# An attention layer's last block: three groups of heads finished in a chain of their own

## What is computed

```
x = x + attention(layernorm(x))     # 16 heads of 16, rotary positions, causal softmax, w_proj and b_proj
x = x + ffn(layernorm(x))
ffn(y) = sqrt((y @ cos(theta + theta_noise))**2 + (y @ sin(phi + phi_noise))**2)
```

## Time and profile before

| | |
|---|---|
| median of 3 runs | 1975.45 us (1974.7 to 1977.72) |
| the profiled execution, own time / span | 1979.04 / 1977.3 us |
| PE busy | 1939.0 us, 98% |
| DVE busy | 1559.9 us, 79% |
| ACT busy | 1389.1 us, 70% |
| POOL busy | 871.0 us, 44% |
| chain that ended last | PE 87%, ACT 5% |
| mean granted TensorE clock | 0.997 |

### The profile page before, as it was taken

How to read it: one execution, slowest core, us unless ns; L and a number is a source line. 1 busy time by engine, 2 the same in 40 slices (tenths; PEclk the granted TensorE clock), 3 DMA queues, 4 the chain that set the end, 5 groups by cost and what they waited for, 6 DMA issues and landing times.

```text
span 1977.3 us, 38203 instructions
## 1 busy us (share of the span) xinstructions
PE 1939.0 (98%) x12036; PEld 798.1 (40%) x12036; DVE 1559.9 (79%) x4101; ACT 1389.1 (70%) x2687; POOL 871.0 (44%) x1336
## 2 busy tenths in 40 slices
PE   7999999999999999999999999999999999999998
PEld 4333433334443434343443443434444344433335
DVE  5898789988778787887877878888777877879725
ACT  3466668877676777877767777777767767777883
POOL 4714615443535454633544435553444545431232
PEclk9999999999999999999999999999999999999999
DMA  6301312122121221311222121322212212120131
GB/s 143 97 24 28 121 47 73 39 71 65 52 73 54 74 83 64 105 35 64 61 71 77 57 72 56 104 68 71 72 33 71 68 64 78 51 94 7 49 105 57
DMA packets 130762, 133.30 MB, mean 67 GB/s; under 512 B 29434, under 2 KB 105722, under 8 KB 130554
## 3 DMA queue, kind: packets, MB, share of 16 engines
q1 hardware_dynamic: 127728, 128.29, 21.1%
q10 hardware_dynamic: 2832, 2.56, 0.7%
HBM read 38.49 MB, written 25.68 MB: 32 GB/s over the span
## 4 chain that ended last, share of the span: by engine, by line
PE 87%; ACT 5%; issue 2%; DVE 2%; DMA 2%; POOL 1%; SPq 0%; DVEq 0%; POOLq 0%; ACTq 0%
PE banks L1094 23%; PE banks L1079 23%; PE banks L1057 22%; PE banks L1012 6%; PE banks L1001 6%; ACT probs L1198 3%; PE banks L1039 3%; PE banks L946 2%; DVE chunk_max L1399 1%; PE banks L935 1%; DMA squares<-sums 1%; PE banks L928 1%; PE banks L1065 0%; DVE banks L1394 0%; PE banks L1024 0%
## 5 line engine op out<-in xcount | busy, mean ns | idle before, releaser
L1198 ACT ACTIVATE probs<-banks 128x512 f32<-128x512 f32 (+1 forms) x2240 | 1143.9, 602 | 328.6 <-PE banks L1079 289.3
L1399 DVE TENSOR_REDUCE chunk_max<-banks 128x1 f32<-128x512 f32 x1536 | 985.3, 683 | 216.7 <-PE banks L1057 215.0
L1079 PE MATMUL banks<-queries,stack_k 99*128 99x512 bf16 (+3 forms) x2560 | 740.5, 350 | 11.8 <-ACT probs L1198 4.1
L1057 PE MATMUL banks<-stack_k,queries 96*128 96x512 bf16 (+3 forms) x2560 | 712.2, 349 | 8.2 <-DMA queries<-parts 2.8
L1394 DVE CUSTOM_DVE_ANT_0 banks<-banks,row_mask 128x128 f32<-128x128 f32 (+3 forms) x1024 | 483.7, 508 | 87.4 <-PE banks L1057 86.8
L1094 PE MATMUL banks<-probs,v_one 128*17 128x512 f32 (+3 forms) x5120 | 527.8, 532 | 1.1 <-POOL probs L1526 0.6
L1079 PEld LDWEIGHTS banks<-queries,stack_k 99*128 99x128 bf16 x2560 | 231.4, 97 | 435.9 <-ACT probs L1198 218.7
L1057 PEld LDWEIGHTS banks<-stack_k,queries 96*128 96x128 bf16 x2560 | 233.0, 97 | 310.9 <-DVE chunk_max L1399 67.3
L1526 POOL TENSOR_SCALAR_AFFINE_SELECT probs<-probs 128x512 f32<-128x512 f32 x256 | 160.9, 638 | 402.5 <-ACT probs L1198 402.0
L1094 PEld LDWEIGHTS banks<-probs,v_one 128*17 128x17 f32 x5120 | 119.7, 96 | 266.3 <-issue 173.7
L1394 DVE DVE_READ_ACCUMULATOR2_ANT chunk_max<- 128x1 f32 x1024 | 144.0, 141 | 0.0
(11 more groups left out here) (158 smaller groups left out, 1162.3 us busy)
## 6 DMA issues: line engine op xcount, KB each, us to landing
queries<-parts SPq DMA_DIRECT2D x384, 64.0 KB, 2.6
stack_k<-parts SPq DMA_DIRECT2D x354, 64.0 KB, 2.6
sums<-o_raw SPq DMA_DIRECT2D x64, 256.0 KB, 2.3
rot<-raw SPq DMA_DIRECT2D x236, 64.0 KB, 2.0
xin<-x SPq DMA_DIRECT2D x17, 512.0 KB, 4.2
mid<-x SPq DMA_DIRECT2D x13, 512.0 KB, 5.1
heads_t<-sums SPq DMA_DIRECT2D x26, 256.0 KB
inverse<-inverses SPq DMA_DIRECT2D x26, 256.0 KB
```

The lines of the kernel that those rows point to most:

```text
L1057: mm = nc.tensor.matmul(bank[:, n * wide:(n + 1) * wide], queries[0:SPLIT_ROWS, query_place(u, t), h + n, j * P:(j + 1) * P], stack_k[u % ...
L1079: mm = nc.tensor.matmul(bank[:, a * wide:(a + 1) * wide], stack_k[u % 2][0:ROWS, j // SUB, first + a, (j % SUB) * P:(j % SUB + 1) * P], qu ...
L1198: nc.scalar.activation(probs[:, g % PROBS, first:first + many, w0:SPAN], bank, ACT.Exp).then_inc(s_exp, 1)
L1399: nc.vector.tensor_reduce(to, bank[:, 0:count * wide].rearrange("p (h n) -> p h n", h=count), AX.X, ALU.max).then_inc(s_emptied["DVE"], 1)
```

## The change

`FINAL`'s early jobs (den, heads, x3, bias, invert, keepinv, inverse, scale, the two leads) are tied in the plan to those of the finish before the last batch (`m = n - SPANS`, number 11) in place of number 14's, and get a due time of their own, `LEAD_AT` = 15.3. They have semaphores of their own, since they now overtake 12, 13 and 14, and the denominators' load waits until `stack_k[0]` is free. No computation is added or taken away.

```diff
+LEAD_AT = 15.3
...
-            job(("den", n), "SP", 0.5, at, [stored, ("power", prev, 1), ("sin", KT - 1), ("den", n - 1), begun(at - SLACK)], 2.2)
...
+            m = n - SPANS if n == FINAL else n - 1
+            at = LEAD_AT if n == FINAL else at
+            job(("den", n), "SP", 0.5, at, [stored, ("power", prev, 1), ("sin", KT - 1), ("den", m), begun(at - SLACK), *(free if n == FINAL else [])], 2.2)
+            job(("heads", n), "SP", 1.5, at, [stored, ("wave", prev, SUB - 1), ("sin", KT - 1), ("heads", m), *free], 2.5)
+            job(("x3", n), "SP", 0.65, at, [("final", prev), ("x3", m), begun(at - SLACK), *free], 4.2)
+            job(("bias", n), "POOL", 2.5, at, [("x3", n), ("bias", m)])
...
+            job(("scale", n), "DVE", 1.25, at, [("heads", n), ("inverse", n), ("scale", m)])
             for a in range(2):
                 first = ("lead" if n == FINAL else "proj", n, a)
-                job(first, "PE", 8 * 4 * DIM / 2 / 2400, at + 0.1, [("scale", n), ("proj", n - 1, 1), ("lead", n, 0) if a else ("scale", n)])
+                job(first, "PE", 8 * 4 * DIM / 2 / 2400, at + 0.1, [("scale", n), ("proj", m, 1), ("lead", n, 0) if a else ("scale", n)])
...
-                job(("weights",), "SP", 0.8, at - 0.4, projected, 3.0)
+                job(("weights",), "SP", 0.8, LAST_AT - 0.4, projected, 3.0)
...
+                    if n == FINAL:
+                        take_late(n)
...
-                    pe.wait_ge(s_scaled, FINAL + 1)
+                    pe.wait_ge(s_lead_scaled, 1)
...
-                        dve.wait_ge(s_bias, n + 1)
+                        if n == FINAL:
+                            dve.wait_ge(s_lead_bias, 1)
+                        else:
+                            dve.wait_ge(s_bias, n + 1)
```

More of the change, by code:

```diff
@@ L337, in plan @@
             stored = ("store", unit - (n == FINAL), t)
-            job(("den", n), "SP", 0.5, at, [stored, ("power", prev, 1), ("sin", KT - 1), ("den", n - 1), begun(at - SLACK)], 2.2)
-            job(("heads", n), "SP", 1.5, at, [stored, ("wave", prev, SUB - 1), ("sin", KT - 1), ("heads", n - 1), *free], 2.5)
-            job(("x3", n), "SP", 0.65, at, [("final", prev), ("x3", n - 1), begun(at - SLACK), *free], 4.2)
-            job(("bias", n), "POOL", 2.5, at, [("x3", n), ("bias", n - 1)])
@@ new lines, in plan @@
+            job(("heads", n), "SP", 1.5, at, [stored, ("wave", prev, SUB - 1), ("sin", KT - 1), ("heads", m), *free], 2.5)
+            job(("x3", n), "SP", 0.65, at, [("final", prev), ("x3", m), begun(at - SLACK), *free], 4.2)
+            job(("bias", n), "POOL", 2.5, at, [("x3", n), ("bias", m)])
+            job(("invert", n), "DVE", 0.5, at, [("den", n), ("invert", m)])
+            job(("keepinv", n), "SP", 0.65, at, [("invert", n), ("keepinv", m)], 2.2)
+            job(("inverse", n), "SP", 1.4, at, [("keepinv", n), ("add", prev), ("inverse", m), *free], 6.8)
@@ L614, in layer_kernel @@
         s_scaled = sem("heads_scaled3")
+        s_lead_bias = sem("last_bias_added")
+        s_lead_inverted = sem("last_denominators_of_first_groups_inverted")
+        s_lead_scaled = sem("last_heads_of_first_groups_scaled")
         s_stat3 = sem("stats_chain3")
@@ L811, in keep_inverses @@
                     f = finish_set(n)
-                    sp.wait_ge(s_inverted, n + 1)
+                    if n == FINAL:
+                        sp.wait_ge(s_lead_inverted, 1)
+                    else:
+                        sp.wait_ge(s_inverted, n + 1)
                     count = heads_by_memory(n)
@@ L1296, in invert @@
                     dve.wait_ge(s_den[f], 16 * (same_set(n)[0] + 1))
-                    nc.vector.reciprocal(denominators[f][rows, :], denominators[f][rows, :]).then_inc(s_inverted, 1)
+                    nc.vector.reciprocal(denominators[f][rows, :], denominators[f][rows, :]).then_inc(s_lead_inverted if n == FINAL else s_inverted, 1)
                 def scale_heads(n):
@@ L1306, in scale_heads @@
                         nc.vector.tensor_tensor(heads_t[f][0:rest_rows, 1, :], heads_t[f][0:rest_rows, 1, :], inverse3[f][0:rest_rows, 1, :],
-                                                ALU.mult).then_inc(s_scaled, 1)
+                                                ALU.mult).then_inc(s_lead_scaled, 1)
                         return
@@ L1492, in add_bias @@
                     nc.gpsimd.tensor_tensor(mid[f][:, :, :], mid[f][:, :, :], bias[:, :].unsqueeze(1).to_broadcast([P, SUB, DIM]),
-                                            ALU.add).then_inc(s_bias, 1)
+                                            ALU.add).then_inc(s_lead_bias if n == FINAL else s_bias, 1)
                 def sum_squares(n, a):
```

## The result

The changed kernel takes 1981.42 us, median of 8 runs (1979.05 to 1984.75), beside 1976.69 us for the kernel before, median of 8 (1974.7 to 1977.72). The ratio is 1.0026, interval 1.0016 to 1.0037: slower by 0.26%. The profiled execution has a span of 1978.6 us.

The account below looks back on a forecast made before the run. PE, busy 98% of the span, was taken as the bound. Leads in the body at +4.58 us and the tail at -0.12 made +4.5 on 1975.45, so 1979.9 us; 8-in-10 range 1977.2 to 1981.8.

Parts of the forecast that it names:

- item 2: Unit 15's span 3 up to the last lift: leads on the path, less 0.34 us of PE idle, +4.58 us.
- item 1: The two leads moved from tail to body: 16 records keep their alternation of rows and take 4.92 us there too.
- The rival's 3.46 us: Leads in the body: 16 records at the like-shape pace of 0.216 us, +3.0 us in all, 1978.5; chance 0.04.
- The reserve of scores in ACT: At the second lead: two waiting score banks give ACT 0.9 us of cover; left out of the sum, kept for the range.
- The sign that misled: Last lift of the changed profile: expected 4 to 5 us later, at 1937; under 3 us later would mean the leads hid.
- Where PE is the limit: From 1886 to 1896, behind the leads: ACT busy 10.00 of 10 us paces PE, so extra PE work would cost little.
- item 3: Tail: 7.02 us out, 6.90 us of 31 dummies in, net -0.12 us; norm 1.6 us early.
- item 4: Unit 15's span 3: seven moved transfers and under 4 us of moved DVE work, hidden by attention, cost nothing.
- The level: Whole kernel: the +4.5 us was put on the runs' median, 1975.45 us, not the profiled execution's 1979.04.
- the fall of the clock behind a wait: Span 3: added DVE work starves PE and the clock drops, +7.0 us, 1982.4; chance 0.07.
- The partly hidden case: Leads in the body: ACT's waiting scores and small gaps hide part, +1 to +3.9 us, 1978.4 at its middle; chance 0.22.
- the faster case: Last two spans: PE's projections and transposes of 13 and 14 come sooner, 4 us to find after 1896, 1971.4; chance 0.04.

## Why the prediction came out as it did

The mechanism was the forecast one, and the time, 1981.42 us, lies in the range, near its upper end. Forecast were 1979.9 us and +4.5; the marks give +4.8 and the medians +4.7. The step that failed is item 2, what lies on the path until the last lift: it said +4.58 us, and the marks show +4.93. The larger part of the miss of the time itself, 1.2 us, is the level on which the sum stood. Point by point:

- **The leads' length (item 1).** 4.92 us taken over from the tail; 2.41 us each in the body, 4.82 together, 0.10 less. Right. The rival's 3.46 us needed the rows to stay alike, and with the rows alike the trace shows just that, 1.73 us a lead. The price of the alternation was attributed rightly.
- **What lies on the path (item 2).** Here a term was mis-sized: "PE has 0.15 and 0.19 us of idle time from 1856 to 1876 that could take some of the 4.92 us. I take all of it, 0.34 us". The last unit grew by 4.93 us where 4.58 were forecast, which is the leads' whole length and 0.11 us more; PE's idle time in it did not shrink by 0.34 us but grew, from 1.40 to 1.87 us. There are two readings, and no run separates them. Either none of the leads hid; or about 0.36 us of them did, much as forecast, and the rest of span 3's new order, which the sum put at nothing, costs the 0.48 us that the kernel with the leads back shows at span 2's diagonal. For the second speaks the wait of 0.55 us that the changed kernel has ahead of its first lead, and the kernel before has not; for the first, that in one order 3.08 us of leads were paid with 2.94. The reserve of scores in ACT, kept for the range, made no difference to the end.
- **The sign that misled.** I wrote that I am wrong if the last lift is under 3 us later. By the profiles' own clocks it is 1.45 us later, 1933.82 against 1932.37, and the end 1.3 us later. The sign took it for granted that the body ahead of unit 15 takes the same time in both executions, and it took 3.5 us less; between the two marks the lift is 4.93 us later.
- **Where PE is the limit.** I wrote that from 1886 to 1896 PE is paced by exponentials, and that extra work on PE "would cost little". That did not enter the sum, but it was wrong: with the leads later, the one there cost 2.1 of its 2.4 us. ACT's 10.00 of 10 us and PE's 9.95 are two engines that are both full, not one that leaves room in the other.
- **The tail (item 3).** -0.12 forecast, -0.1 measured, and the kernel with 22 dummies shows that it is PE's stream. The norm was ready 2.15 us ahead, 1.6 forecast, in part since the way from DVE's last statistic to ACT's norm took 2.73 us (1944.69 to 1947.42) against the 3.25 of the earlier trace rows.
- **Transfers and moved work (item 4).** Nothing was forecast, and DVE's scale of the last block did not wait for its inverses: SP issued them at 1833.87 and the scale ran at 1846.66. With all this moved and the leads back, both stretches together take 144.80 us, as before; the 0.48 us above are inside that.
- **The level.** The sum stood on 1975.45 us. Beside the changed kernel the kernel before measured 1976.69, and this makes 1.2 of the 1.5 us between forecast and result.

Of the rivals, the fall of the clock behind a wait did not come with this change, but came when the dummies were taken away. The partly hidden case was not the case here; with the leads elsewhere up to 1 us may have hid. In the faster case the price was put on gaps in the body; the room for 4 us lay in the tail's order instead, which that rival did not look at.

## What to carry to other kernels

On an engine that is full, work moved out of the tail gains only if the tail's stream becomes shorter; look first at what the scheduler puts in its place, here 22 more dummy matmuls for 16 records of work. Compare two kernels between two marks of the program, not by their spans, where the clock falls in some executions and not in others. A sign that is to tell whether a forecast failed has to be written between such marks too. A busy neighbour is no proof that an engine has room: add up one step of both.

## What the runs showed of the hardware

- A change between matmuls of 128 and of 64 rows costs about 0.09 us for each record of 256 columns in fp32 in an alternating stream: 0.30 against 0.216 us. With the matmuls grouped, two changes fewer, a lead of 8 records took 2.02 us in place of 2.41.
- With a wait of PE of 4.67 us the granted clock fell 0.3 us ahead of the wait's end and was at half for 3.4 us, and a wave of 1.72 us took 2.82.
- A GpSimd mask of 0.63 us took 1.68, 0.94 and 0.79 us when it met a VectorE operation with two inputs in SBUF, and ended 0.49 to 0.50 us behind it each time.
